# The experts' results are added into the output itself instead of into a scratch table

## The reference

```python
x = x + _L1_gnn_ref(_layernorm(x), L1_gnn_W, L1_gnn_b, edge_index)
# _L1_ffn_ref on the layer-normed x: softmax over 8 experts, the best two, weights normalised
#   h = gelu(xe @ W1[e] + b1[e]);  y = h @ W2[e] + b2[e]        (256 -> 1024 -> 256)
#   out[row] = w1 * y[best expert] + w2 * y[second expert]
x = x + _L1_ffn_ref(_layernorm(x)[None], ...)[0]
return x                                                       # 6250 x 256
```

## Time and profile before

| what | value |
|---|---|
| median of three runs | 3413.09 us |
| profiled execution, own time | 3406.11 us |
| its span in the trace | 3404.5 us |
| PE busy, all | 2389.7 us, 70% |
| POOL busy, all | 1914.0 us, 56% |
| DVE busy, all | 1530.2 us, 45% |
| ACT busy, all | 826.3 us, 24% |
| moved by DMA, all | 298.25 MB |
| granted PE clock, mean | 0.814 |

### The profile page before, as it was taken

The page is one execution under the profiler, slowest core; times in us unless marked ns, Lnnn a source line. Parts: engine busy times, 40 slices in busy tenths (PEclk is TensorE's granted clock), DMA queues, the critical chain, the costliest instruction groups (busy, mean ns, idle before and its releaser), DMA issues. The chain is left out here.

```text
span 3404.5 us, 48482 instructions
## 1 busy us (share of the span) xinstructions
PE 2389.7 (70%) x12359; PEld 1580.8 (46%) x12360; DVE 1530.2 (45%) x4138; ACT 826.3 (24%) x1644; POOL 1914.0 (56%) x2043
## 2 busy tenths in 40 slices
PE   1389988998867777553665565544356689999996
PEld 1255555555433343231332232221123279999996
DVE  7455555555542433032554534322232156666663
ACT  2234333333312211020110000000000045555543
POOL 0364555556666656526666666676655455555553
PEclk6589999989877878775677676665678789999998
DMA  5222222223233232223333333333322443333334
GB/s 167 88 83 62 75 75 83 81 85 87 78 90 91 82 87 85 83 80 91 91 93 95 96 95 91 95 100 91 99 82 71 123 115 71 73 73 72 72 49 106
DMA packets 163078, 298.25 MB, mean 88 GB/s; under 512 B 47543, under 2 KB 106656, under 8 KB 162752
## 3 DMA queue, kind: packets, MB, share of 16 engines
q0 software_dynamic: 96736, 235.19, 26.6%
q1 hardware_dynamic: 41476, 39.54, 3.7%
q10 hardware_dynamic: 24732, 22.06, 2.1%
HBM read 255.78 MB, written 47.27 MB: 89 GB/s over the span
## 5 line engine op out<-in xcount | busy, mean ns | idle before, releaser
L760 POOL DMA_INDIRECT rows<-table,srcT x1568 | 1543.2, 984 | 988.5 <-issue 460.1
L862 PE MATMUL bank<-rows,onehot 128*128 x1952 | 633.6, 450 | 569.3 <-issue 343.5
L810 DVE SCALAR_TENSOR_TENSOR onehot<-iota_row,tbase,dstT 128x512 f16 x488 | 366.6, 753 | 770.9 <-issue 434.3
L862 PEld LDWEIGHTS bank<-rows,onehot 128*128 x1952 | 207.0, 106 | 956.3 <-issue 823.1
L2023 ACT ACTIVATE hid<-bank,b 128x256 f32<-128x256 f32 x432 | 179.3, 466 | 291.6 <-PE bank L1975 266.0
L1973 PE MATMUL bank<-W_high,hid_high 128*128 128x256 f32 x864 | 244.9, 283 | 0.0
L1973 PE MATMUL bank<-xe_high,W_high 128*128 128x256 f32 x864 | 241.0, 279 | 5.2 <-DVE xe_low L2056 5.2
L1975 PE MATMUL bank<-xe_high,W_low 128*128 128x256 f32 x864 | 240.0, 278 | 0.0
L1974 PE MATMUL bank<-W_low,hid_high 128*128 128x256 f32 x864 | 240.0, 278 | 0.0
L1974 PE MATMUL bank<-xe_low,W_high 128*128 128x256 f32 x864 | 239.9, 278 | 0.0
L1975 PE MATMUL bank<-W_high,hid_low 128*128 128x256 f32 x864 | 239.9, 278 | 0.0
(11 more groups left out here) (355 smaller groups left out, 3903.9 us busy)
## 6 DMA issues: line engine op xcount, KB each, us to landing
rows<-table,srcT POOLq DMA_INDIRECT x1568
W<-in_L_ffn_W_dram SPq DMA_DIRECT2D x14, 1024.0 KB
x_res<-in_x_dram SPq DMA_DIRECT2D x1, 6144.0 KB, 22.2
normal<-xn ACTq DMA_DIRECT2D x11, 528.0 KB
table<-part ACTq DMA_DIRECT2D x11, 512.0 KB
totals<-x_res SPq DMA_DIRECT2D x11, 512.0 KB, 6.9
table<-part SPq DMA_DIRECT2D x6, 512.0 KB, 2.9
table<-part_b SPq DMA_DIRECT2D x6, 512.0 KB, 2.9
```

Source lines behind the costliest of these rows:

```text
L760: nc.gpsimd.indirect_dma_start(out=rows[:, k % (M * U), 0:ROW], out_offset=None, in_=q.table, in_offset=bass.IndirectOffsetOnAxis(srcT[:, ...
L810: last = nc.vector.scalar_tensor_tensor(onehot[:, ds(slot, U), :], iota_row[:, :].unsqueeze(1).to_broadcast([P, U, P]), base, dstT[:, ds(k ...
L862: last = nc.tensor.matmul(acc[:, 0:ROW], hots[:, ds(hot0 + s * P, P)], ring_rows[:, ds(row0 + s * ROW, ROW)], start=False, stop=False, ski ...
```

## The change: what it does

The table `totals` is gone. SP stores `x_res` to the output. The 13 groups of whole tiles behind the first go as before; the group of the last tile (the first that is stored) is cut to the 106 rows that exist. The zero fill goes. The scatters of `ys` add into the output, and carry a bound: an index above 6249 (`N - 1`) is left out without an error. These are the numbers of empty slots, from 6272 up, and those of the 22 padding rows, 6250 to 6271. `totals_begun` counts 14 DMAs instead of 15. The copies at the end go, and SP waits for `all_out` itself.

```diff
-        totals = nc.dram_tensor("totals", (NPAD + TT, D), F32).ap()
@@ the second graph layer, SP
-                sp.dma_start(totals[NPAD:NPAD + TT, :].rearrange("(s p) d -> p s d", p=P),
-                             zeros[:, :].unsqueeze(1).to_broadcast([P, SUB, D])).then_inc(X["totals_begun"], 16)
                 sp.wait_ge(q2.done, NT)
                 for g in range(LAST + 1):
                     t, w = first_tile(g), size(g)
                     sp.wait_ge(R["xn_ready"], g + 1)
-                    sp.dma_start(totals[t * P:(t + w) * P, :].rearrange("(t p) d -> p t d", p=P),
-                                 x_cols(t, w).rearrange("p (t d) -> p t d", d=D)).then_inc(X["totals_begun"], 16)
+                    whole = min(t + w, NT - 1) - t
+                    if whole:
+                        sp.dma_start(out[t * P:(t + whole) * P, :].rearrange("(t p) d -> p t d", p=P),
+                                     x_cols(t, whole).rearrange("p (t d) -> p t d", d=D)).then_inc(X["totals_begun"], 16)
+                    else:
+                        sp.dma_start(out[t * P:N, :], x_res[0:N - t * P, t * D:(t + 1) * D]).then_inc(X["totals_begun"], 16)
@@ the experts
-        def copied_out(eng, first, last):
-
-            eng.wait_ge(X["all_out"], 1)
-            for r0 in range(first, last, W):
-                r1 = min(r0 + W, last)
-                k = GW if r1 - r0 == W else 1
-                eng.dma_start(out[r0:r1, :].rearrange("(p k) d -> p (k d)", k=k),
-                              totals[r0:r1, :].rearrange("(p k) d -> p (k d)", k=k)).then_inc(X["copied_out"], 16)
@@ SP, at its end
-                copied_out(sp, 0, GROUPS // 2 * W)
-                sp.wait_ge(X["copied_out"], 16 * (GROUPS + 1))
+                sp.wait_ge(X["all_out"], 1)
@@ POOL
                         nc.gpsimd.indirect_dma_start(
-                            out=totals, out_offset=bass.IndirectOffsetOnAxis(to_old[:, s:s + 1], axis=0),
-                            in_=ys[:, s, :], in_offset=None, compute_op=ALU.add).then_inc(X["y_out"], 16)
+                            out=out, out_offset=bass.IndirectOffsetOnAxis(to_old[:, s:s + 1], axis=0),
+                            in_=ys[:, s, :], in_offset=None, compute_op=ALU.add,
+                            bounds_check=N - 1, oob_is_err=False).then_inc(X["y_out"], 16)
@@
-                    pool.wait_ge(X["totals_begun"], 16 * (LAST + 2))
+                    pool.wait_ge(X["totals_begun"], 16 * (LAST + 1))
@@ ACT, at its end
-                copied_out(act, GROUPS // 2 * W, N)
```

## The result

The changed kernel takes 3409.18 us (median of 20 runs, 3392.93 to 3429.23), the kernel before 3420.98 us in the same comparison (20 runs, 3406.27 to 3440.78). The ratio is 0.9945, 95% interval 0.9926 to 0.9963: 18.8 us less, between 13 and 25. I had forecast 3390.7 us in a range of 3384 to 3401, 22.4 us less. The direction was right, and the time lies outside the range.

What follows compares the result with a forecast made beforehand. PE sets the loop's length, then comes an end only DMA works in. Copies -21.9 and zero fill -0.5 sum to -22.4 us; 3413.1 - 22.4 = 3390.7 us, range 3384 to 3401.

Steps and rivals of the forecast that it cites:

- the first: End of the span: without the copies SP waits for `all_out` at 3382.29 and the span ends at 3382.58, -21.9 us.
- an earlier last landing: Last scatter, with fewer transfers: landing at most from 2.37 us to 1.8 us, -0.6 to 0.
- my signs of being wrong: Scatters' median above 2.1 us, PE's loop idle beyond 5 us, or something copied or waited for behind the last scatter.
- The bound: Loop's scatters: bound adds 0.0 to 0.3 us each, taken as 0; up to 0.5 hidden, except 1 us at the end.
- A: Loop's scatters: bound adds 0.5 to 1.2 us each and eats part; at 0.8, 3400.0 us; chance 0.07.
- B: Loop: POOL becomes the bound, gain gone at a scatter of 2.83 us, 3456 us at the upper end; chance 0.07.
- The target: Scatters adding into the output instead of `totals`: cost taken as 0.
- rival C: Scatters' landings: the output takes adds more slowly, +1 to +9 us, 3392 to 3400 us; chance 0.04.
- The zero fill: Before the second graph layer's first gather: without the fill `frees` comes 0 to 1.16 us earlier; taken as -0.5 us.
- The store of 106 rows: Stores ahead of the first scatter: cost 0 under 10 us of cover, 0 to +2 for delaying other transfers.
- the rule on engines: Cut store: SP's DMA uses the largest engine number up to 16 dividing 106, so 2; 2.5 us instead of 0.4.
- Rival D: End of the span: something else sets it, so nothing is saved; chance 0.02.

Runs made afterwards that it cites:

- e1: The changed kernel with POOL's DRAIN at the end of the last block left out: 3376.23 us, ratio 0.9932 to the kernel before.
- e4: The kernel before with only the first two of the 13 copies at the end, the rest of the output unwritten: 3383.12 us, ratio 0.9964.
- e9: The changed kernel once more, unaltered, in a later group of runs: 3185.48 us, ratio 0.9951 to the kernel before.
- e10: The changed kernel without POOL's last drain, run once more beside e9: 3178.79 us, ratio 0.9930 to the kernel before.
- e6: The changed kernel with the 256 KB zero fill kept, into a table nothing reads; PE's mean clock was 0.545, span 3986.5 us.

## Why the prediction was wrong, point by point

**The step that failed** is the first: "With the same 0.29 us behind the last wait the span ends at 3382.58", and "What is late next is the last scatter". I took the 0.29 us for a constant. It was what was left when SP came last and all other engines had finished their ends long before. POOL's drain of 7.32 us was the next in line, in the trace before and under the cover that the change removes. I had looked at busy rows, and this view names queue instructions only when asked for the block's line. The worked-out gain with it is 24.58 - 9.06 = 15.5 us, 6.4 less than 21.9: 7.3 lost to the drain and 1.1 given back by an earlier last landing, a term that I had bounded at 0.6; the 0.2 left are in the hand-overs before and behind the drain. It was also the one of my signs of being wrong that came true: something is waited for behind the last scatter.

**The base.** Most of the rest of the miss is not the change. My 3390.7 stood on 3413.09, a median of three runs; twenty gave 3420.98, 7.9 us more. With both, 3413.1 + 7.9 - 15.5 = 3405.5, against 3409.2 measured; the 3.7 us between lie in the spread of the runs and are not explained. "Runs of this kernel differ by up to 10 us" was too small: the twenty differ by 34.5 us. In four profiles of one chip the last stage begins between 2707.1 and 2734.9 us, with the same code ahead of it in the last three (e1 to e4: 2720.2, 2734.9, 2724.8, 2707.1; e1 has neither fill nor whole first store). A range of 17 us on an absolute time was too narrow for that, though as a difference my forecast of -22.4 is inside the interval of 13 to 25. That is luck and not the mechanism: the ends of the traces give 15.5, and e9's interval leaves 22.4 out.

**The bound.** I took 0, 0 to 0.3 expected, and 0.5 us as free. The median did not move; the mean rose 0.11 us, by a start 0.09 us later that decides which of two engines waits, most of it from the 29 ns move in front of each scatter. It cost nothing in the loop (644.33 and 644.25 us), as the slack of 1.05 to 2.40 us a tile said. Rivals A and B did not come; B's knee of 2.83 us a scatter is far off.

**The target** (rival C) cost nothing that shows: the last landing is shorter, DVE's waits for landings are 23.0 us in the changed kernel and 18.3 in e9 against 19.2, and e9's gain agrees with its end to 0.2 us. **The zero fill**: the profiles give 0.3 us of the 0.5 in the mean, and do not tell it from nothing. My sign for it, a first gather that waits 5.5 to 6.7 us, was missed at 7.07; other profiles without the fill have 6.09 to 6.37. **The store of 106 rows** did no harm: POOL's gap ahead of the first scatter is 1.16 us, against 1.04, about the 0.09 more that stand ahead of the other tiles' scatters too. Its landing is not in the trace after, so the rule on engines that the prediction cites was neither shown nor refuted. **Rival D**, that something else sets the end, I gave 0.02 with "I see no room for it"; a third of it was true.

## What to carry to other kernels

Before a tail is cut, list for each engine when it reaches its last instruction *including* the drains and barriers of the block's end, and take the next latest as the new end, not the old one minus the wait. Here a long last transfer hid what another queue still did, and its removal was worth the distance to the next in line. Where an engine's drain is that next thing and all of its DMAs have been waited for, ask for the end without it: here that was another 7.3 us in the trace and 6.7 in the runs of e9 and e10.

## What the runs showed of the hardware

POOL's DRAIN at a block's end took the same time in every profile, and a different one by block: 1.87 to 1.88 us at the end of the first, 4.65 and 4.63 at the ends of the two graph layers, and 7324 to 7327 ns at the end of the last stage, in all nine profiles that have it. At the end of the last stage it did not depend on whether the scatters had a bound, where they went, what ran beside it, or PE's clock (7327 ns at 0.545 too). What it is spent on no run here tells. PE's took 2.0 us and DVE's 0.86 us there, both long hidden.

A `hid_low` operation of DVE that starts 0.045 to 0.13 us ahead of a scatter made the scatter 2.0 to 2.1 us instead of 1.62; with a smaller lead DVE's own took up to 0.77 instead of 0.69. A bound set by a register move of 29 ns ahead of each scatter was enough to take the scatters of 2 us and more from 3 to 28 of 112.

One chip took 3399 us for the kernel before and two others 3198 and 3200, at mean granted clocks of 0.81 to 0.82 and 0.83 to 0.84; its loop over experts took 642.8 to 647.3 us on all three (e6 apart), so the 200 us lie ahead of it.
